# Self attention of a two-layer decoder: scores kept in PSUM, the mask added by TensorE, softplus by two routes, four row tiles, and keys rotated on GpSimd

## What is computed

```python
q = (X @ Wq + bq)   # 64 heads, rotated by position
k = (X @ Wk + bk)   # 16 heads, repeated for the 4 branches, rotated
v = (X @ Wv + bv)   # 64 heads
scores = einsum('bhtd,bhsd->bhts', q, k) * 16 ** -0.5
w = softplus(scores / sqrt(clip(sum(k * k), 1e-6)))
w = where(causal, w, 0)
w = w * sigmoid(pi / sqrt(3) * w)
alpha = 1 / (sum(w) + tanh(sink) + 2e-6)
out = (w * alpha) @ v + (tanh(sink) + 1e-6) * alpha * v_null
y = mean over the branches of (out @ Wo + bo)
x = layernorm(x + y)
```

## Time and profile before

| | us |
|---|---|
| median of 3 runs | 3083.02 |
| lowest, highest | 3065.78, 3084.93 |
| the profiled execution | 3084.47 |
| its span | 3082.7 |
| the stage "sa" in it | from 37 to 735 |
| one body with all parts | 41.0 |

### The profile page before, as it was taken

One profiled execution on the slowest core, in us unless ns is written; L12 is line 12 of the kernel. 1 busy time (PEld: TensorE's weight loads), 2 busy tenths in 40 slices (PEclk: granted clock), 3 DMA queues, 4 the chain that ended last, 5 costly groups with the idle time before them and its releaser, 6 DMA issues. The chain is left out here.

```text
span 3082.7 us, 44584 instructions
## 1 busy us (share of the span) xinstructions
PE 2467.7 (80%) x15278; PEld 1459.9 (47%) x15279; DVE 1723.8 (56%) x3404; ACT 1187.7 (39%) x2418; POOL 433.1 (14%) x360
## 2 busy tenths in 40 slices
PE   3777777774999999876777489999999999994793
PEld 1333333332666666553444145554455544553572
DVE  3899999993555555534777234444544454453123
ACT  1666666663333333222444124343343433440110
POOL 1333333220111111002343000000000000001102
PEclk9888888885999999977787699999999999995897
DMA  3000000000000000200000200000000000006111
GB/s 110 1 1 0 0 0 0 0 0 27 13 13 10 14 10 10 68 4 9 0 0 0 72 5 11 5 5 5 5 10 5 5 5 5 5 1 229 40 32 51
DMA packets 50289, 60.41 MB, mean 20 GB/s; under 512 B 9764, under 2 KB 44889, under 8 KB 49770
## 3 DMA queue, kind: packets, MB, share of 16 engines
q1 hardware_dynamic: 47218, 53.69, 5.5%
q0 software_dynamic: 3008, 5.91, 0.7%
HBM read 51.06 MB, written 8.52 MB: 19 GB/s over the span
## 5 line engine op out<-in xcount | busy, mean ns | idle before, releaser
L1880 PE MATMUL la_side<-la_wkv,la_inT 128*128 128x512 f32 (+1 forms) x512 | 258.0, 627 | 49.2 <-DVE la_v L2004 48.3
L2138 ACT ACTIVATE la_pr<-la_pS,la_nm 100x461 f32<-100x461 f32 x256 | 163.1, 644 | 267.9 <-DVE la_nm L2041 267.9
L1868 PE MATMUL la_side<-la_inT,la_wkv 128*128 128x461 f32 x512 | 240.1, 592 | 7.6 <-ACT la_kT L2125 6.9
L2038 DVE TENSOR_REDUCE la_nm<-la_pS 100x2 f32<-100x922 f32 x128 | 142.7, 1115 | 182.9 <-PE la_pS L1899 182.9
L300 PE MATMUL sa_pS<-sa_qT,sa_kTm 128*100 128x400 f32 x512 | 195.1, 504 | 7.3 <-DVE sa_L L471 7.3
L2004 DVE COPY la_v<-la_side 128x512 f32<-128x512 f32 (+1 forms) x128 | 87.7, 685 | 180.1 <-PE la_side L1880 180.0
L895 PE MATMUL ca_pS<-ca_kT,ca_qTm 128*100 128x361 f32 x512 | 187.0, 488 | 0.5 <-DVE ca_va L974 0.5
L1075 ACT ACTIVATE ca_pr<-ca_pS,ca_nm 100x361 f32<-100x361 f32 x256 | 129.7, 559 | 125.2 <-DVE ca_nm L1009 125.1
L1006 DVE TENSOR_REDUCE ca_nm<-ca_pS 100x2 f32<-100x722 f32 x128 | 116.3, 908 | 96.6 <-PE ca_pS L895 96.5
L604 ACT ACTIVATE sa_L<-sa_L 100x800 f32<-100x800 f32 x128 | 111.3, 870 | 146.8 <-DVE sa_L L471 146.8
L1880 PEld LDWEIGHTS la_side<-la_wkv,la_inT 128*128 128x128 f32 (+1 forms) x512 | 82.3, 180 | 163.6 <-DVE la_v L2004 91.5
(11 more groups left out here) (385 smaller groups left out, 4924.1 us busy)
## 6 DMA issues: line engine op xcount, KB each, us to landing
rf_w<-in_L_ffn_W SPq DMA_DIRECT2D x16, 1024.0 KB, 13.3
ca_cn<-in_ctx SPq DMA_DIRECT2D x16, 256.0 KB, 2.7
la_cn<-in_ctx SPq DMA_DIRECT2D x16, 256.0 KB, 2.7
rows_in<-io_zero SPq DMA_DIRECT2D x20, 128.0 KB, 4.6
rb_xr<-rows_in POOLq DMA_DIRECT2D x20, 128.0 KB, 2.2
rows_out<-rb_yr SPq DMA_DIRECT2D x20, 128.0 KB, 1.7
ea_wc<-in_L_ffn_conv_W SPq DMA_DIRECT2D x1, 2048.0 KB
la_wkv<-in_L_xattn_Wkv SPq DMA_DIRECT2D x1, 2048.0 KB
```

Of the source, the lines that this page charges most:

```text
L1868: last = nc.tensor.matmul(pf[:, 0:SK], wkv[:, k, e * P:(e + 1) * P], inT[:, k, :], start=k == 0, stop=k == KD - 1)
L1880: last = nc.tensor.matmul(pf[0:keys[c], :], inT[:, k, c * P:c * P + keys[c]], wkv[:, k, o:o + 512], start=k == 0, stop=k == KD - 1)
L2038: nc.vector.reduce_max(nm[m % 2][:], pS[0:T, 2 * (m % 2):2 * (m % 2) + 2, 0:SK], AX)\
L2138: ins = nc.scalar.activation(pr[m % 2][:, e, 0:SK], pS[0:T, 2 * (m % 2) + e, 0:SK], ACT.Exp, bias=nm[m % 2][:, e:e + 1], scale=SCALE, accu ...
```

## The change

Scores stay in PSUM until the softplus is done. A body works on four groups u of four heads each; each head of a group has 32 rows (two heads of 16, of which `odd`, a mask of two columns that also carries the factor 1/4, keeps one), so `scores` is called for half a group: two heads into banks 0 and 1 (half 0), two into banks 2 and 3 (half 1). The causal mask is first put into each bank by a bfloat16 product of an identity and `cmask`, over 100 rows, and the product of keys and queries, over one row tile of 32, is added to it. A half may be computed again when VectorE has done its softplus of the group before: there is one buffer.

Half 0 goes the old way in smaller pieces: minimum with 30 (`bounded`), exponential, logarithm, and the maximum with the score in PSUM. Half 1 goes by another: ScalarE takes the absolute value from PSUM, the exponential of its negative and the logarithm, and VectorE adds the positive part of the score in PSUM. The separate addition of the mask and the tile `sm` are gone. `out_read` goes from ScalarE to VectorE. Rotating, squaring and scaling the keys goes from VectorE to GpSimd, ahead of and between the two halves of rotating the queries. `k_projected` and `q_projected` stand one behind the other near the head of a body; the projection of the values is cut in two, stands between the scores of the groups 1 and 2, and belongs to batch o+2 in place of o+3; `xT` and the keys get a second buffer. The output weights are loaded by four transfers in the order of the new head layout, so 17 transfers are waited for at the start in place of 14.

The diff, cut to its core:

```diff
+odd = sb("odd", [P, 2])
...
+xT = [sb(f"xT{b}", [P, KD, T]) for b in range(2)]
...
-sm = sb("sm", [T, KD, HG, NBR, T])
-L = sb("L", [T, 2, KD, HG, NBR, T])
+kTm = [sb(f"kTm{b}", [P, KD, 2, T]) for b in range(2)]
+L = sb("L", [T, 2, KD, 2, NT, NBR, T])
...
+                 (wo[0:64, 0, :], wo_rows[0, 0]), (wo[64:P, 0, :], wo_rows[0, 1]),
+                 (wo[0:64, 1, :], wo_rows[1, 0]), (wo[64:P, 1, :], wo_rows[1, 1])):
...
-def q_projected(f):
-    above(pe, s_v, f)
+def q_projected(f, par):
+    above(pe, s_qT, f)
...
 def q_turned(f):
     pe.wait_ge(s_qr, f + 1)
-    pe.wait_ge(s_qn, f + 1)
+    above(pe, s_v, f)
...
-def v_projected(f):
-    pe.wait_ge(s_qT, f + 1)
...
+def v_projected(s, par, F, n):
+    if n == 0:
+        if F:
+            pe.wait_ge(s_qn, s + 2)
+        else:
+            pe.wait_ge(s_qT, s + 1)
+            above(pe, s_v, s)
...
+def scores(s, par, u, half):
+    g, p = u // 2, u % 2
+    if u == 0 and half == 0:
         pe.wait_ge(s_kT, s + 1)
         pe.wait_ge(s_qT, s + 1)
-    above(pe, s_sm, s * HG + (m - 1))
-    g, h = m // 4, 2 * (m % 4)
-    for e in range(2):
-        last = nc.tensor.matmul(pS[0:T, 2 * (m % 2) + e, 0:NBR * T], kTm[:, g, h + e, :],
-                                qT[:, g, :, :], start=True, stop=True)
+    above(pe, s_sp, s * HG + (2 * u - 1 + half))
+    for j in range(2 * half, 2 * half + 2):
+        nc.tensor.matmul(pS[0:T, j, 0:NU], identb[:, :], cmask[:, :, :], start=True, stop=False)
+    for j in range(2 * half, 2 * half + 2):
+        tile = slice(QR * j, QR * (j + 1))
+        last = nc.tensor.matmul(pS[0:T, j, 0:NU], kTm[par][tile, g, p, :], qT[tile, g, :, :],
+                                start=False, stop=True)
     last.then_inc(s_S, 1)
...
     F, S, V, O = parts(o)
     f, s, v = o + 3, o + 2, o + 1
     vp = (par + 1) % 2
+    if S:
+        scores(s, par, 0, 0)
+        scores(s, par, 0, 1)
     if O:
         context_turned(o)
-    if S:
-        scores(s, 0)
     if F:
         x_turned(f)
-    if S:
-        scores(s, 1)
     if O:
         out_projected(o)
-    if S:
-        scores(s, 2)
+    if F:
+        k_projected(f, vp)
+        q_projected(f, vp)
     if V:
         values(v, vp, 0)
-    if F:
-        k_projected(f)
     if S:
-        scores(s, 3)
+        scores(s, par, 1, 0)
     if V:
         values_turned(v, 0)
     if S:
-        scores(s, 4)
+        v_projected(s, par, F, 0)
+        scores(s, par, 1, 1)
     if V:
         values(v, vp, 1)
     if F:
-        q_projected(f)
+        k_turned(f)
+    if S:
+        scores(s, par, 2, 0)
     if V:
         values_turned(v, 1)
     if S:
-        scores(s, 5)
+        v_projected(s, par, F, 1)
+        scores(s, par, 2, 1)
     if V:
         values(v, vp, 2)
     if S:
-        scores(s, 6)
+        scores(s, par, 3, 0)
     if V:
         values_turned(v, 2)
     if S:
-        scores(s, 7)
-    if F:
-        k_turned(f)
+        scores(s, par, 3, 1)
     if V:
         values(v, vp, 3)
+        values_turned(v, 3)
     if F:
         q_turned(f)
-    if V:
-        values_turned(v, 3)
-    if F:
-        v_projected(f)
...
+def k_biased(f):
+    dv.wait_ge(s_kp, f + 1)
+    above(dv, s_kq, f)
+    nc.vector.tensor_tensor(kn[:], pk[0:T, 256:512], bk[:], ALU.add).then_inc(s_kn, 1)
...
+def k_summed(f):
     ck.start(f)
+    dv.wait_ge(s_kq, f + 1)
+    above(dv, s_kf, f)
     ck.after(nc.vector.reduce_sum(kss[:], ksq[:, :].rearrange("p (h c) -> p h c", h=NH), AX))
     nc.vector.tensor_scalar(kss[:], kss[:], 1e-6, None, ALU.max).then_inc(s_ks, 1)
...
     kk = pk[:, 0:KD * T].rearrange("p (k t) -> p k t", k=KD)
     nc.vector.tensor_tensor(
-        kTm[:, :, :, :], kk.unsqueeze(2).broadcast_to([P, KD, HG, T]),
-        hmask[:, :].unsqueeze(1).unsqueeze(3).broadcast_to([P, KD, HG, T]), ALU.mult).then_inc(s_kT, 1)
-def v_biased(f, par):
-    dv.wait_ge(s_vp, f + 1)
+        kTm[par][:, :, :, :], kk.unsqueeze(2).broadcast_to([P, KD, 2, T]),
+        odd[:, :].unsqueeze(1).unsqueeze(3).broadcast_to([P, KD, 2, T]), ALU.mult).then_inc(s_kT, 1)
...
+def bounded(s, par, u, o):
+    if u == 0:
         above(dv, s_av, o * 4 + 4)
+    dv.wait_ge(s_S, s * HG + (2 * u + 1))
+    nc.vector.tensor_scalar(half_of(par, u, 0), pS[0:T, 0:2, 0:NU], 30.0, None, ALU.min)\
+        .then_inc(s_lo, 1)
+def softplus(s, par, u, half):
+    dv.wait_ge(s_L, s * HG + (2 * u + half + 1))
+    w = half_of(par, u, half)
+    if half == 0:
+        ins = nc.vector.tensor_tensor(w, w, pS[0:T, 0:2, 0:NU], ALU.max)
+    else:
+        ins = nc.vector.scalar_tensor_tensor(out=w, in0=pS[0:T, 2:4, 0:NU], scalar=0.0, in1=w,
+                                             op0=ALU.max, op1=ALU.add)
+    ins.then_inc(s_sp, 1)
+def out_read(v, c):
+    g, n = c // 2, v * 4 + c
+    dv.wait_ge(s_oNp, n + 1)
+    nc.vector.tensor_copy(oN[:, g, 2 * (c % 2):2 * (c % 2) + 2, :, :].rearrange("p r h c -> p (r h c)"),
+                          pb[0:T, :]).then_inc(s_oN, 1)
...
 def body(o, par):
     F, S, V, O = parts(o)
     f, s, v = o + 3, o + 2, o + 1
+    if S:
+        bounded(s, par, 0, o)
     if O:
         context_read(o)
-    if S:
-        masked(s, par, 0, o)
     if F:
-        xT_read(f)
-    if S:
-        masked(s, par, 1, o)
+        xT_read(f, (par + 1) % 2)
     if O:
         residual(o)
+    if F:
+        k_biased(f)
+        q_biased(f)
+        k_summed(f)
     if S:
-        masked(s, par, 2, o)
-    if F:
-        k_roped(f)
+        softplus(s, par, 0, 0)
+        bounded(s, par, 1, o)
+    if V:
+        out_read(v, 0)
     if S:
-        masked(s, par, 3, o)
+        softplus(s, par, 0, 1)
     if O:
         normed(o)
     if S:
-        masked(s, par, 4, o)
+        softplus(s, par, 1, 0)
+        bounded(s, par, 2, o)
     if F:
-        q_biased(f)
-        k_scaled(f)
+        kT_read(f, (par + 1) % 2)
     if S:
-        masked(s, par, 5, o)
-        softplus(s, par, 0)
+        softplus(s, par, 1, 1)
     if V:
+        out_read(v, 1)
+    if S:
+        softplus(s, par, 2, 0)
+        bounded(s, par, 3, o)
+        v_biased(s, par)
+        softplus(s, par, 2, 1)
+    if V:
+        out_read(v, 2)
         norm(v, 0)
     if S:
-        masked(s, par, 6, o)
-        masked(s, par, 7, o)
-    if F:
-        kT_read(f)
+        softplus(s, par, 3, 0)
+    if V:
+        out_read(v, 3)
+    if S:
+        softplus(s, par, 3, 1)
     if V:
         norm(v, 1)
-    if S:
-        softplus(s, par, 1)
-    if F:
-        v_biased(f, (par + 1) % 2)
...
+nc.vector.tensor_copy(cmask[:], causal[:, :].unsqueeze(1).broadcast_to([T, NBR, T])).then_inc(s_d0, 1)
+nc.vector.tensor_copy(identb[:], ident[0:T, 0:T]).then_inc(s_d0, 1)
...
+def logs_of_bounded(s, par, u):
+    n, w = s * HG + 2 * u, half_of(par, u, 0)
+    ac.wait_ge(s_lo, s * 4 + (u + 1))
+    nc.scalar.activation(w, w, ACT.Exp).then_inc(s_E, 1)
+    ac.wait_ge(s_E, n + 1)
+    nc.scalar.activation(w, w, ACT.Ln, bias=1.0).then_inc(s_L, 1)
+def logs_of_abs(s, par, u, o):
+    n, w = s * HG + 2 * u + 1, half_of(par, u, 1)
+    if u == 0:
+        above(ac, s_av, o * 4 + 4)
+    ac.wait_ge(s_S, n + 1)
+    nc.scalar.activation(w, pS[0:T, 2:4, 0:NU], ACT.Abs).then_inc(s_ab, 1)
+    ac.wait_ge(s_ab, s * 4 + (u + 1))
+    nc.scalar.activation(w, w, ACT.Exp, scale=-1.0).then_inc(s_E, 1)
+    ac.wait_ge(s_E, n + 1)
+    nc.scalar.activation(w, w, ACT.Ln, bias=1.0).then_inc(s_L, 1)
+def gate(v, par, g):
+    ac.wait_ge(s_sp, v * HG + 4 * (g + 1))
+    w = L[:, par, g].rearrange("t p j r q -> t (p j r q)")
...
+    if S:
+        logs_of_bounded(s, par, 0)
     if V:
         values_read(v, 0)
     if S:
-        exponential(s, par, 0)
+        logs_of_abs(s, par, 0, o)
+    if F:
+        k_factors(f)
     if O:
...
         values_read(v, 3)
+    if S:
+        logs_of_abs(s, par, 3, o)
     if F:
         qT_read(f)
-    if V:
-        out_read(v, 3, o)
-    if S:
-        exponential(s, par, 7)
-        logarithm(s, par, 1)
...
+def k_roped(f):
+    po.wait_ge(s_kn, f + 1)
...
+    for n, (x, y_) in enumerate(((0, c), (1, s), (0, s), (1, c))):
+        nc.gpsimd.tensor_tensor(A[n], h[:, :, :, x], y_, ALU.mult).then_inc(s_pk, 1)
+    po.wait_ge(s_pk, f * 6 + 4)
+    above(po, s_kTp, f)
+    nc.gpsimd.tensor_tensor(o[:, :, 0:DH // 2], A[0], A[1], ALU.subtract).then_inc(s_pk, 1)
+    nc.gpsimd.tensor_tensor(o[:, :, DH // 2:DH], A[2], A[3], ALU.add).then_inc(s_pk, 1)
+    po.wait_ge(s_pk, f * 6 + 6)
+    above(po, s_ks, f)
+    nc.gpsimd.tensor_tensor(ksq[:], kr[:], kr[:], ALU.mult).then_inc(s_kq, 1)
+def k_scaled(f):
+    po.wait_ge(s_kf, f + 1)
+    o = kr[:, :].rearrange("p (h c) -> p h c", h=NH)
+    nc.gpsimd.tensor_tensor(o, o, kf[:, :].unsqueeze(2).broadcast_to([T, NH, DH]), ALU.mult)\
+        .then_inc(s_kr, 1)
...
 def body(o, par):
     F, S, V, O = parts(o)
-    if O:
-        residual(o)
     if F:
         staged(o + 3)
-        q_roped(o + 3)
+        k_roped(o + 3)
+        q_roped(o + 3, 0)
+        k_scaled(o + 3)
```

(6 more changed lines are left out.)

210 lines of the change are left out of this document (78 added, 132 removed).

## The result

The kernel after takes 3126.21 us (median of 4 runs, 3123.46 to 3140.52), the kernel before 3077.56 in its 4 runs beside them. The ratio is 1.0175, 95% interval 1.0133 to 1.0217: slower by 49 us, where I forecast 3072 and no change.

What follows compares the result with a forecast made beforehand. VectorE, 38.05 of 41.0 us a body, was taken as the bound. A 38.05 us chain plus clock loss made 40.5; 14 bodies saved 7 us, the start 4: 3073.5 profiled, 3072 us forecast, range 3052 to 3092, 8 in 10 3022 to 3130.

Steps and rivals of the forecast that it cites:

- VectorE sets the pace: Kernel before, stage "sa": VectorE, busy 38.05 us of a 41.0 us body, was taken as what bounds it.
- The sum's last operation +0.9: VectorE's sum of the keys' squares, before the first softplus: drawn out beside GpSimd's first query operation, +0.9 us (none to 1.1).
- GpSimd 18: GpSimd's busy time per body with the keys' work added: 18 us of 41, where it had 12.9.
- A half of the scores 1.35: TensorE, two mask and two key products with row tiles side by side: 1.35 us with load and signals.
- The rival with tiles in series: Score tiles not side by side: +0.65 us on each of six halves, body 42 us, 3094 to 3110; chance 0.05.
- a price of 0.2 for each switch: Rival: each switch from whole rows to row tiles costs, 1 to 1.2 us a body, 3087 us; chance 0.10.
- The chain at full clock, 38.05: One body's path from last softplus to last softplus, each scores half awaiting the softplus before: 38.05 us against 41.0.
- step 1: Head of the chain: norm, context, output, key and query projections, query bias, squares' sum, first softplus, ending at 14.0 us.
- The clock: TensorE falls to half clock after two gaps, +2.4 and +0.7 us, part given back: 40.5 us a body.
- the query projection at half clock: Rival: clock still low in the next body's head; 42.9 us a body, 3106, or 44.5 and 3128; chance 0.25.
- The sum: Whole execution: 14 bodies gain 0.5 us each, 7 us, plus 4 at the start: 3072 us.
- The signs: Listed checks: body 40 to 41 us, VectorE near 27, ScalarE near 28, stated waits for TensorE, clock below 0.88.

Runs made afterwards that it cites:

- before_keys: Kernel before with only the keys' rotation, squares and scaling moved to GpSimd, their factors one place later on ScalarE: 3071.89 us, 0.9978 of before.
- before_fill: Kernel before with 26 added products, results unread, on TensorE ahead of the turn of the queries: 3075.88 us, 0.9992 of before.
- fill_all: Kernel after with added TensorE products, results unread, in three gaps of a body (16, 12 and 5): 3040.67 us, 0.9902 of before.

## Why the prediction was wrong

- *What bounds the kernel before.* "VectorE sets the pace" was only half right. It is the longest engine, but not the whole path: 2.6 us less of it gave 0.75 (before_keys). TensorE's clock is not what holds this kernel either: raised from 0.88 to 0.93 it gave nothing (before_fill).
- *The engines after.* VectorE about 27: 27.2. ScalarE about 28: 28.5. The minimum from PSUM at the high end, 0.98: 0.988; by that the rule of the Trainium skill cited there ("VectorE: DVE Perf Modes", "Why PSUM operands drop a tier") agrees with the trace. The absolute value 0.87: 0.841. The sum's last operation +0.9: 1.04, where L431, the same operation before, took 0.175. GpSimd 18 was wrong, it is 12.4: 3.1 of the 5.6 are L713, which I kept at 4.42; its successor L744 takes 1.29, with no operation of 3200 columns beside it. The rest is spread over the other operations, and the prediction's own terms (12.9, 3.6 and 0.7) make 17.2 and not 18.
- *A half of the scores 1.35.* Masks from 392.42, scores from 392.85 for 0.92: 1.35. The rival with tiles in series (a pair over 1.3) falls. So does that of a price of 0.2 for each switch: the scores start 0.43 after the masks, where 0.24 + 0.17 were counted without one. The Trainium skill ("TensorEngine Tiling (Array Packing)", "Key Properties") says that a change of the tiling mode drains TensorE; these rows leave 0.02 us for it, and other halves of this body, whose scores start 0.47 to 0.48 after the masks, some 0.07.
- *The chain at full clock, 38.05.* The full-clock body of fill_all has 36.7: 13.2, 17.2, 23.6 and 30.3 where the steps give 14.0, 18.1, 24.6 and 31.1 at the same softplus operations. 0.8 too long in step 1, the rest right to 0.2 up to the softplus of group 2, and 0.6 too long at the end.
- ***The clock* is the step that failed.** It found both gaps and the falls behind them. It took 40.5 us on the assumption that the clock is up again for the head of the next body. It is not: it stays at half from the scores (3, 1) to the first products of the query projection, 17 us, and the scores of group 0, output and key projection lie in them. That is 3.7 us a body in step 1, where the step had nothing. Behind step 1 it had 2.4 and 0.7, of which 0.65 were given back; measured 2.8 and 1.2, and nothing given back. So 36.7 + 3.7 + 4.0 = 44.4, where the forecast was 38.05 + 2.45.
- *The rival "the query projection at half clock"* named this mechanism, with the scores of group 0 that hold the context back (1.1, measured 1.7) and the projections at half. Its 44.5 us and 3128 are close to the 44.4 and 3126 by errors that cancel: it had the clock low until the queries are done, and it comes back at their first products; the base was 1.4 too long. Its terms, 1.1 and up to 4.6 on 40.5, make up to 46.2, and no working gives the 44.5. And it counted from 3083, where the kernel before took 3077.56 in the runs beside. I gave it 0.25 and had no row for the assumption that I preferred.
- *The sum.* 14 x 0.5 us gained were 3.3 x 14 = 46 lost. Of the 4 us at the start, in which a longer setup was already counted, 1.6 were there: 24 us from the stage's start to the first scores, in place of 28, but a start 2.4 us later. And the partial bodies, three counted as one, lost about as much each as the full ones, the first 7.7 us.
- *The signs.* The body of 40 to 41 us did not come. L465 of group 1 waited 2.6 us for TensorE, not 1.4, and ScalarE's copies (L617) 1.7 to 4.5, not 1.5 to 2. VectorE and ScalarE, the first softplus behind L433 and L434, and a clock below 0.88 (0.73) came as said; those signs fit the right rival as well as the forecast.
